# Attention and gated FFN on one core: the pass for the score maxima by single PSUM banks, the end with turned sums, and the orders of a period refitted

## The reference

```
q = rotary(xn @ wq + bq), k = rotary(xn @ wk + bk), v = xn @ wv + bv     16 query heads, 2 groups of k and v, 16 wide
attention = softmax(q k^T / 16) v @ wo + bo                              over 1024 keys
ffn = fwht(silu(xn @ W1^T) * (xn @ W3^T)) @ W2^T                         1024 hidden units, fwht = normalised Walsh-Hadamard
```

## Time and profile before

| | us |
|---|---|
| median of 3 runs | 1078.76 |
| lowest, highest | 1078.07, 1084.82 |
| profiled execution, its own time | 1075.6 |
| its span | 1073.8 |
| PE, VectorE, ScalarE, GpSimd busy | 1014.3, 771.2, 707.5, 347.2 |
| granted share of the TensorE clock, mean | 0.99 |

### The profile page before, as it was taken

One profiled execution on the slowest core, in us unless ns is written; L12 is line 12 of the kernel. 1 busy time (PEld: TensorE's weight loads), 2 busy tenths in 40 slices (PEclk: granted clock), 3 DMA queues, 4 the chain that ended last, 5 costly groups with the idle time before them and its releaser, 6 DMA issues.

```text
span 1073.8 us, 19578 instructions
## 1 busy us (share of the span) xinstructions
PE 1014.3 (94%) x7604; PEld 549.6 (51%) x7604; DVE 771.2 (72%) x934; ACT 707.5 (66%) x1336; POOL 347.2 (32%) x300
## 2 busy tenths in 40 slices
PE   4889999999999999999999999999999999999997
PEld 3554445545554555545554455545555454644454
DVE  5996688677776778767786777767776778776723
ACT  4256677657765777657776577667775678566873
POOL 5262722073312634054310735126320224012300
PEclk9998999999999999999999999999999999999999
DMA  8762155212052253402242250521123131510001
GB/s 234 177 172 75 53 137 104 74 57 86 17 117 78 76 136 66 100 21 84 64 103 74 97 126 18 117 64 51 51 62 71 33 83 33 111 32 6 12 8 50
DMA packets 64941, 84.03 MB, mean 78 GB/s; under 512 B 19960, under 2 KB 34168, under 8 KB 64848
## 3 DMA queue, kind: packets, MB, share of 16 engines
q1 hardware_dynamic: 63296, 80.74, 29.1%
q10 hardware_dynamic: 1552, 2.03, 0.7%
HBM read 54.97 MB, written 22.51 MB: 72 GB/s over the span
## 4 chain that ended last, share of the span: by engine, by line
PE 66%; DVE 17%; ACT 5%; issue 4%; DMA 4%; SPq 3%; POOL 2%; DVEq 0%; ACTq 0%; POOLq 0%
PE ps L1501 16%; PE ps L1558 14%; PE ps L1545 13%; DVE negpart L1295 11%; PE ps L1456 9%; PE ps L1513 8%; PE ps L1467 3%; DVE hid L1267 3%; PE ps L1434 3%; ACT work L1079 2%; DMA qk_parts<-hid 1%; DMA xn<-in_x 1%; SPq L776 1%; SPq L784 1%; DMA recip_rows<-dens 1%
## 5 line engine op out<-in xcount | busy, mean ns | idle before, releaser
L1295 DVE TENSOR_REDUCE negpart<-ps 128x2 f32<-128x1024 f32 x512 | 619.0, 1224 | 235.7 <-PE ps L1456 234.8
L1079 ACT ACTIVATE work<-ps 128x512 f32<-128x512 f32 x1024 | 560.0, 603 | 262.3 <-PE ps L1545 256.9
L1558 PE MATMUL ps<-work,vb 128*32 128x512 f32 x2048 | 274.6, 609 | 5.8 <-ACT osum L1090 5.0
L1545 PE MATMUL ps<-qh,kb 50*128 50x512 f32 x1024 | 265.1, 450 | 10.3 <-ACT work L1079 7.4
L1456 PE MATMUL ps<-kb,qh 48*128 48x512 f32 x1024 | 226.8, 433 | 9.6 <-DVE negpart L1295 5.3
L1545 PEld LDWEIGHTS ps<-qh,kb 50*128 50x128 f32 x1024 | 123.4, 185 | 212.3 <-ACT work L1079 159.0
L1501 PE MATMUL ps<-xf,w_p 64*128 64x512 f32 x1536 | 218.3, 400 | 7.4 <-DVE negpart L1295 1.4
L1501 PEld LDWEIGHTS ps<-xf,w_p 64*128 64x128 f32 x1536 | 143.6, 185 | 49.7 <-DVE hid L1267 16.3
L933 POOL TENSOR_TENSOR hid_p<-hid,hid_p 128x512 fp32r<-128x512 f32 x64 | 82.2, 1286 | 203.1 <-ACT hid_p L1068 203.1
L1456 PEld LDWEIGHTS ps<-kb,qh 48*128 48x128 f32 x1024 | 98.1, 185 | 82.7 <-DVE negpart L1295 48.4
L1513 PEld LDWEIGHTS ps<-w2t_p,hid_p 64*128 64x128 f32 x1536 | 107.7, 185 | 34.2 <-DVE negpart L1295 27.1
(11 more groups left out here) (125 smaller groups left out, 484.6 us busy)
## 6 DMA issues: line engine op xcount, KB each, us to landing
xf<-xn_parts SPq DMA_DIRECT2D x32, 512.0 KB, 8.5
qh<-qk_parts SPq DMA_DIRECT2D x192, 64.0 KB, 2.3
xn_parts<-xt SPq DMA_DIRECT2D x14, 512.0 KB, 3.5
qh<-mturned SPq DMA_DIRECT2D x256, 2.0 KB
y<-in_x SPq DMA_DIRECT2D x8, 512.0 KB, 4.8
attnt<-osum SPq DMA_DIRECT2D x124, 32.0 KB, 2.0
recips<-recip_rows SPq DMA_DIRECT2D x120, 32.0 KB, 1.8
xn<-in_x SPq DMA_DIRECT2D x7, 512.0 KB, 5.0
```

The costliest lines, as they stand in the source:

```text
L1079: nc.scalar.activation(prob[(ITSTEPS * i + j) % NPROB][:, h, :], ps[:, 4 + u % 3, :], ACT.Exp, scale=SCALE).then_inc(exp_done, 1)
L1295: nc.vector.tensor_reduce(negpart[a][:, f, :, h, t, e], two(slot), AX.X, ALU.max, negate=True).then_inc(ring_free[slot], 1)
L1545: pe.matmul(ps[:, 4 + u % 3, :], kb[i % 2][rows, kt * P:(kt + 1) * P], qh[2 * a + f][rows, h, :], start=True, stop=True).then_inc(s2_done, 1)
L1558: m = pe.matmul(ps[VW * h:VW * (h + 1), 7, :], vb[b % 2][g][:, kt, :], prob[(ITSTEPS * i + j) % NPROB][:, h, :], start=(kt == 0), stop=(kt ...
```

## The change

1. **Maxima by single banks.** An S1 entry has two pieces, two fills and two frees. Piece 0 is the product for r = 1, piece 1 that for r = 0. Each fills one bank; VectorE takes one maximum of 128x512 for each, in the same order. Piece 0 waits only for the first free of an S1 unit before it in the slot, piece 1 for the second.
2. **Other products between them.** `first(slot, *halves)` issues the named pieces, so that `first(1, 0)`, something else, `first(1, 1)` puts scores or own pieces between the two products of a unit.
3. **Orders refitted.** PE's order of each kind of period is written anew, and where exponentials, tanh, copies and saves lie on ScalarE. VectorE's order in a period is the same, with two maxima for each unit.
4. **Last iteration.** UP ends at period 9, DN runs in periods 11 to 14, and period 15 (WOz) projects the first half of iteration 7's own sums. Reciprocals of half 0 are taken at period 12 there.
5. **The end.** The last copy of the sums, `select` and `chosen` go. VectorE turns the sums out of PSUM in blocks of 32x32 (queries onto partitions), takes reciprocals of 128x8, multiplies, turns back; both in halves of 256. PE gathers the four head blocks' output in banks 2 to 5: first the part of the normalised half from `attnt`, then the part of the turned one, against rows of `wo` (`wo_last`, zero in the denominators' rows; a memset on GpSimd and four DMAs in iteration 6). Two additions of 128x512 follow.

The diff, cut to its core (kinds WO, XT, None, WOx, QKx, UPxo and the first two periods of the kernel are rewritten in the same manner):

```diff
 def up_at(i):
-    return range(4, 12) if i + 2 < NBLK else (1, 2, 3, 5, 6, 7, 8, 10)
+    return range(4, 12) if i + 2 < NBLK else (1, 2, 3, 5, 6, 7, 8, 10 if i + 1 < NIT else 9)
+def down_at(i):
+    return range(12, 16) if i + 1 < NIT else range(11, 15)
...
-PIECES = {"XT": 2, "QK": 4, "Q2": 2, "WO": 4, "UP": 4, "DN": 4, "VT": 1, "S1": 1}
-FULLS = {"XT": 2, "QK": 2}
-FREES = {"XT": 2, "UP": 2, "VT": 2}
+PIECES = {"XT": 2, "QK": 4, "Q2": 2, "WO": 4, "UP": 4, "DN": 4, "VT": 1, "S1": 2}
+FULLS = {"XT": 2, "QK": 2, "S1": 2}
+FREES = {"XT": 2, "UP": 2, "VT": 2, "S1": 2}
...
         if kind in ("UP", "UPo"):
-            own(0, 1)
-            first(1)
+            own(0)
+            first(1, 0)
+            own(1)
+            first(1, 1)
             scores(0)
             sums_before()
+            first(1, 0)
             scores(1)
-            first(1)
-            own(2)
+            first(1, 1)
+            own(2, 3)
+            first(1, 0)
             scores(2)
-            own(3)
-            first(1)
+            first(1, 1)
             sums(i, 2 * p)
+            first(1, 0)
             scores(3)
-            first(1)
+            first(1, 1)
         elif kind in ("DN", "DNo"):
             scores(0)
-            first(0)
-            first(1)
+            first(0, 0, 1)
+            first(1, 0, 1)
             sums_before()
-            own(0)
             scores(1)
-            first(1)
+            own(0)
+            first(1, 0)
             own(1)
+            first(1, 1)
             scores(2)
+            first(1, 0)
             own(2)
-            first(1)
-            scores(3)
+            first(1, 1)
             own(3)
+            scores(3)
             sums(i, 2 * p)
...
         elif kind == "QK":
+            first(1, 0)
             scores(0)
-            first(1)
-            first(0)
+            first(1, 1)
             scores(1)
+            first(0, 0, 1)
+            sums_before()
+            sums(i, 2 * p)
             scores(2)
-            sums_before()
-            own(0)
-            first(1)
-            own(1, 2, 3)
-            first(1)
-            sums(i, 2 * p)
+            first(1, 0, 1)
+            own(0, 1, 2)
+            first(1, 0)
             scores(3)
+            first(1, 1)
+            own(3)
             extra()
...
+        elif kind in ("WO", "WOo"):
+            first(1, 0), scores(0), first(1, 1), scores(1), first(1, 0), scores(2), first(1, 1)
+            own(0, 1, 2, 3), scores(3), first(1, 0, 1), sums_before(), first(0, 0, 1), sums(i, 2 * p)
+        elif kind == "XT":
+            first(1, 0), scores(0), first(1, 1), own(0, 1), scores(1), first(1, 0, 1), sums_before()
+            scores(2), first(1, 0), scores(3), first(1, 1), first(0, 0, 1), sums(i, 2 * p)
...
-                dve.wait_ge(*filled(("S1", i, a, u)))
...
-                nc.vector.tensor_reduce(negpart[a][:, f, :, h, t, e], two(slot), AX.X, ALU.max,
-                                        negate=True).then_inc(ring_free[slot], 1)
+                for n, r in enumerate((1, 0)):
+                    dve.wait_ge(*filled(("S1", i, a, u), n + 1))
+                    nc.vector.tensor_reduce(negpart[a][:, f, r, h, t, e:e + 1], two(slot)[:, r, :], AX.X, ALU.max,
+                                            negate=True).then_inc(ring_free[slot], 1)
...
-                if k == 0 and RING[entry][2] > 0:
+                if k == 0 and RING[entry][3] > 0:
+                    pe.wait_ge(ring_free[slot], RING[entry][3])
+                if k == 1 and RING[entry][2] > RING[entry][3]:
                     pe.wait_ge(ring_free[slot], RING[entry][2])
...
-                    for r in range(ROWT):
-                        rows = slice(GRP * r, GRP * r + SROWS)
-                        m = pe.matmul(bank[:, r, :], ...)
+                    r = ROWT - 1 - k
+                    rows = slice(GRP * r, GRP * r + SROWS)
+                    m = pe.matmul(bank[:, r, :], ...)
+                    done = True
...
                     if kind == "UP":
                         exponentials(i, j, 0, 4)
                         hidden_before(i, p)
+                        gate(i, up_at(i).index(p))
                         exponentials(i, j, 4, 5)
-                        gate(i, up_at(i).index(p))
-                        exponentials(i, j, 5, 6)
                         linear(i, up_at(i).index(p))
-                        exponentials(i, j, 6, 8)
+                        exponentials(i, j, 5, 8)
...
+            for n, cols in enumerate(halves):
+                nc.vector.transpose(last_sums[:, cols], ps[:, 7, cols]).then_inc(last_turned, 1)
+            for n in range(2):
+                nc.vector.reciprocal(shares[n], blocks[n][:, :, HD]).then_inc(last_step, 1)
+            for n in range(2):
+                nc.vector.tensor_tensor(blocks[n][:, :, 0:HD], blocks[n][:, :, 0:HD],
+                                        shares[n].unsqueeze(2).broadcast_to([P, 2 * P // VW, HD]), ALU.mult).then_inc(last_step, 1)
+            for n, cols in enumerate(halves):
+                nc.vector.transpose(last_attn[:, cols], last_sums[:, cols]).then_inc(last_norm, 1)
```

More of the change, by code:

```diff
@@ L135, in sums_before, with first @@
             sums(i - 1, ITSTEPS - 1)
-    def first(slot):
+    def first(slot, *halves):
         nonlocal unit
[L139 to L142, removed]
+        for n in halves:
+            at = i + unit // (2 * UNITS)
+            if at < NIT:
+                piece(("S1", at, unit // UNITS % 2, unit % UNITS), n, slot)
+            unit += n
     def own(*numbers):
@@ new lines, in walk_iteration @@
+            own(3)
+            scores(3)
+            extra()
+            first(1, 0, 1)
+        elif kind == "UPxo":
+            first(0, 0, 1)
+            first(1, 0)
+            scores(0)
+            first(1, 1)
+            scores(1)
+            own(0)
+            first(1, 0)
+            scores(2)
+            first(1, 1)
+            own(1, 2)
+            scores(3)
+            own(3)
+            first(1, 0, 1)
+            sums_before()
+            extra()
+            sums(i, 2 * p)
+        elif kind == "Nos":
+            first(0, 0)
+            scores(0)
+            first(0, 1)
+            sums_before()
+            scores(1)
+            scores(2)
+            first(0, 0)
+            scores(3)
+            first(0, 1)
+            first(1, 0, 1)
+            sums(i, 2 * p)
+            first(0, 0, 1)
+        elif kind == "Not":
+            first(1, 0)
+            scores(0)
+            first(1, 1)
+            scores(1)
+            first(0, 0)
+            scores(2)
+            first(0, 1)
+            scores(3)
+            first(1, 0, 1)
@@ L265, in walk_iteration @@
             sums_before()
-            first(0)
-            first(1)
+            first(1, 0, 1)
+            sums(i, 2 * p)
+        elif kind == "WOz":
             scores(0)
             scores(1)
-            own(0, 1, 2, 3)
+            own(0, 1)
             scores(2)
-            sums(i, 2 * p)
-            first(1)
+            own(2, 3)
             scores(3)
[L275 to L297, removed]
@@ L342, in walk_opening, with walk_closing @@
         piece(("UP", 0, c), k, 2 + c % 2)
-def walk_closing(sums, piece, select):
+def walk_closing(sums, piece, last_values):
     sums(NIT - 1, ITSTEPS - 1)
-    select()
-    for half in range(QB):
-        for k in range(4):
-            piece(("WO", NIT - 1, half), k, 1 - half)
+    last_values()
 def ring_table():
-    full, free, at = [0] * 4, [0] * 4, {}
+    full, free, at, before = [0] * 4, [0] * 4, {}, [None] * 4
     def count(entry, k, slot):
         if k == 0:
-            at[entry] = (slot, full[slot], free[slot])
+            at[entry] = (slot, full[slot], free[slot], free[slot] - (entry[0] == before[slot] == "S1"))
+            before[slot] = entry[0]
             full[slot] += FULLS.get(entry[0], 1)
@@ L1197, in _ @@
+                        exponentials(i, j, 4, 5)
+                        linear(i, up_at(i).index(p))
+                        exponentials(i, j, 5, 8)
+                    elif kind == "DNo":
+                        exponentials(i, j, 0, 1)
+                        hidden_before(i, p)
+                        exponentials(i, j, 1, 3)
+                        save_finished(i, p)
+                        exponentials(i, j, 3, 8)
+                    elif kind == "WOo":
                         exponentials(i, j, 0, 4)
@@ L1424, in _ @@
-            projected_sums(NIT - 1, 0)
-            for n in range(2):
-                at = y[:, (NBLK - 1) % 2, 2 * n:2 * n + 2, :].rearrange("p t d -> p (t d)")
-                dve.wait_ge(*filled(("WO", NIT - 1, 1), n + 1))
-                nc.vector.tensor_tensor(at, at, two(0)[:, n, :], ALU.add).then_inc(ring_free[0], 1)
+            halves = [slice(n * 2 * P, (n + 1) * 2 * P) for n in range(2)]
+            blocks = [last_sums[:, cols].rearrange("p (j c) -> p j c", c=VW) for cols in halves]
```

243 lines of the change are left out of this document (118 added, 125 removed).

## The result

| | before | changed |
|---|---|---|
| median of the runs | 1079.63 | 1095.25 |
| lowest, highest | 1078.07, 1084.82 | 1087.58, 1098.10 |
| profiled execution, span | 1075.6, 1073.8 | 1092.8, 1091.0 |
| mean granted clock, profiled execution | 0.990 | 0.955 |

In 37 other executions of the kernel before (1075.8 to 1088.9 us) the mean clock was 0.976 to 0.989, in 32 of them 0.984 or less, so the profiled one, at 0.990, is among its fastest. The ratio is 1.012 (95% interval 1.008 to 1.016): slower by about 1%, where 1041 us and faster were forecast, and outside the range of 1020 to 1072.

What follows compares the result with a forecast made beforehand. PE and VectorE were taken to wait for each other in a loop through one buffer. Terms of -22.5 - 3.8 - 10.7 - 2.5 - 4.5 + 1.7 = -42.3, plus 5 for what was missed, gave -37: 1041 us, range 1020 to 1072.

Steps and rivals of the forecast that it cites:

- XT + QK: XT and QK periods of a steady iteration: about 6.3 and 10.9 us, together 17.2, for 15.94 and 1.4 moved in.
- WO + WOx: WO and WOx periods of a steady iteration: 7.8 and 9.3 us, together 17.1, for 17.98.
- UP: UP periods of a steady iteration: 7.35 us each for 7.58, counted as 7 x 7.35 + 5.5.
- DN: DN periods of a steady iteration: 7.45 us each, four taking 29.8 for 32.93, of which 1.4 moves into the next period.
- Q2's stall: QK period: Q2 writes the slot the second projection must read first, a stall of 1.05 us.
- the gated product's: UP periods: VectorE's late gated product leaves PE a stall of 0.27 us, plus 0.10.
- (d): Rival: each split product shows a weight load, 390 x 0.10 = +39, no change, 1080 us; chance 0.05.
- The opening: 24 units back to back, where the split maxima are not hidden: 24 x 0.07 = +1.7 us.
- The end: From the last sums to the end of the last addition: 5.3 us for 9.83, so -4.5.
- (b): Rival: the new orders eat the gain through waits in Q2, scores and periods, 30 us back, 1070 us; chance 0.20.
- (c): Rival: a single product leaves the other row half idle, 390 x 0.23 = +90 for -37, 1130 us; chance 0.05.
- (a): Rival: the refit clears the gated wait too, UP periods come to 6.98 us, -20, 1020 us; chance 0.18.

Runs made afterwards that it cites:

- e1: Changed kernel with SyncE's eight loads of the next iteration's first maxima put ahead of spreading the reciprocals: 1044.7 us, 0.968 of the kernel before.
- e3: Kernel before with split products and split maxima alone, both products together where the pair was, old orders and old end: 1087.49 us, 1.007.
- e6: Changed kernel with the 2 MB load of the turned x moved from ahead of the reciprocals to behind the maxima's loads: 1050.01 us, 0.969.
- e8: Changed kernel, maxima's loads between the reciprocals' write and the wait for it, both products of a unit together at the second's place: 1082.96 us, 1.000.
- e9: Changed kernel, maxima's loads between the reciprocals' write and the wait for it, one QK sums moved between own(3) and extra(): 1041.74 us, 0.962.
- e10: e9 with the gated product between the third unit's maxima and, between UP periods, the fourth unit's second product behind the next own(0): 1039.29 us, 0.959.
- e5: Kernel before with the six loads of queries put ahead of the eight loads of the first maxima on SyncE: 1147.53 us, 1.062.
- e2: Kernel before with the same swap as e1, the first maxima's loads ahead of spreading the reciprocals: 1079.25 us, 0.998.

## Why the prediction was wrong, point by point

**Steps that held.** For a steady iteration, forecast against e1, where the border is cured: XT + QK 17.2 and 16.95; WO + WOx 17.1 and 17.08; UP 57.0 and 57.41; DN 29.8 and 29.60 (there by an offset: 7.9 for the first and 7.2 for the others, where each was put at 7.45); sum 121.1 and 121.0. The maxima are 0.685 us long and two take 1.29, so 0.60 apart. Q2's stall and the gated product's are where they were put. The mechanism of the split was read rightly. e1's 1044.7 lies 4 us from the forecast, with some luck: from the last DN period of iteration 5 to the end e1 gains 14.0 us on the profiled kernel before, where the sum has 19.2 (10.7, the 1.5 counted elsewhere, 2.5 and 4.5), and the 5 us added for what was missed cover just that.

Two arguments of the prediction have to be put right. The Trainium skill (VectorE: DVE Perf Modes, "The DRAIN you can't avoid") goes on, behind the sentence that the prediction cites, with an exception: "A next op that is not held starts earlier", held being its word for one that starts only when all earlier ones have finished. Starts 1.131 us apart at a length of 1.23, and 0.60 apart at 0.685, agree with that exception, so the trace does not disagree with the section as a whole.

The other is that on weight loads in the same rows, against rival (d). The six full-height products 0.22 apart in the earlier trace rows have 256 columns, and pairs of DN products of as many columns stand 0.12 apart there, so that row by itself leaves time for a load in the open. What bears the argument out are the products of the projection in QK of the kernel before, also full-height, each with its own load, and of 512 columns:

```profile
460.09 1.22 PEld L1434 LDWEIGHTS ps<-xt,wqkv_p 128*128 128x128 f32 x6 [0.25 <-issue]
460.09 1.67 PE L1434 MATMUL ps<-xt,wqkv_p 128*128 128x512 f32 x6
```

Six take 1.67 us, just what six pairs of half-height UP products take behind a stall, 0.23 apart, and their first and last load lie within 1.22 us: no load between them shows. What holds the products of 256 columns at 0.22 is open.

**The step that failed** is DN: "Four take 29.8". They would have, but the end of an iteration is not PE's alone. I followed what PE, VectorE and ScalarE hand each other, and costed SyncE by what the edit adds to it ("on a queue with gaps"). I never asked what that queue delivers at the border and by when. Counted from the write of the reciprocals, the border came 1.3 us sooner (2.5 at the last two), and the chain that the maxima's loads stand behind (write, landing, eight spreading DMAs) did not get shorter with PE's periods but 2.2 us longer, for the most part because the write moved closer behind the turned x. The kernel before met this date within 0.4 us at five borders of seven. Here PE stood still for 2.4 to 4.7 us at each border, 23.8 in all, and the last DN period came to 10.1 to 12.4 us instead of 7.2.

**The clock, not in the sum at all.** The mean granted clock of 0.955 means some 98 us at 1.2 GHz of 1091 (2 x 0.045 x 1091), against 21 in the profiled execution before and 46 in e1. With a stall of 2.4 to 4.7 us at a border it fell for 3 to 14 us, at three of them once more within the iteration, and XT, QK and WO then ran at half speed. A stall on PE thus cost about twice its length: 1091.0 minus 1043.9 is 47 us over seven borders, 6.7 each, 3.4 of them stall. The other 23 us would be, by this working, the price of the 52 us more at half the clock (98 less 46). Part of the clock's falls is not of this kind. The changed kernel has one of 17 us in the opening, near 45 us, about 1 us behind a gap of 2.05 us without products, and e1, e3, e6, e8, e9 and e10 have it too. So does e5, with the old units. The profiled execution of the kernel before has a gap of 1.87 us there and no such fall. So it isn't a matter of single banks. Nor does the kernel seem to settle it: ten executions of e2, old units too, have a clock of 0.991 to 0.992 (two of them, at 1074.4 and 1074.8 us) or 0.980 to 0.986 (eight, at 1078.1 to 1083.3); what falls in those eight no trace shows. What decides it was not tried.

**The opening** cost 5.3 us (first score at 78.4 for 73.1), where +1.7 was forecast. This fall of the clock is enough for all of it: e5, with the old maxima and the same fall, has its first score at 78.6, and the runs with single maxima and this fall have it at 77.2 to 78.9. So the +1.7 for the split maxima does not show in any run.

**The end** held within a little. In the changed kernel:

```profile
1082.61 0.13 PEld L1596 LDWEIGHTS ps<-work,vb 128*32 128x32 f32 x4 [0.30 <-issue]
...
1083.72 0.78 DVE L1452 STREAM_TRANSPOSE work<-ps 128x256 f32<-128x256 f32 x2 [1.94 <-PE ps L1596]
1084.42 0.31 DVE L1455 RECIPROCAL work<-work 128x8 f32<-128x8 f32 x2
1084.66 0.46 DVE L1458 TENSOR_TENSOR work<-work 128x128 f32<-128x128 f32 x2
...
1087.62 0.69 DVE L1466 TENSOR_TENSOR y<-y,ps 128x512 f32<-128x512 f32 x1 [0.18 <-PE ps L1611]
```

The last `sums` begins with the load at 1082.61 and the last addition ends at 1088.31: 5.7 us, forecast 5.3, before 9.83. The turns take 0.78 a pair, where 0.75 was put; the reciprocals and products 0.31 and 0.46, where 0.4 and 0.5 were put.

**The rivals.** None was the one that came, and none had the time: the nearest, (d), was put at 1080. The sign named for (b), iterations of 124 us and more, did appear (127.9 from 586.08 on), and yet not for its reason: it put the loss into PE's orders. (c) and (d) are out: e1's UP periods of 7.38 leave no room for 0.11 a split. (a) did not come true either; e10 shows that the gated wait is not the only one between 7.38 and 6.98. The iterations with WOo (6 and 7) were off as well: WOo takes 10.0 in e1 at its shortest, and I had 8.2.

## What to carry to other kernels

Before a stretch is made shorter, list all that is due at its end, DMAs that another queue issues above all, and take from the trace how long before its use each arrives; a row with a wait of 0.3 us for a DMA, or a last issue that is always just one landing ahead, is a date that is met by chance. A small load that something waits for goes ahead of the large one that is needed later, and the write whose landing the queue itself waits for goes there too, as long as the large one still comes in time (e6). When a gain doesn't show, compare the same stretches by period kind before doubting the edit: here the eight UP periods had their gain all along (57.41 us for 58.75), and two swapped calls brought the rest.

## What the runs showed that was not expected

Stalls of PE for 2.4 to 4.7 us came with half the granted clock for 3 to 14 us at a time; in e5, with stalls of 5.1 us at six borders and 3.9 at the last, it was 7 to 21 us, and 17 or more at four of the seven. A write of 16 KB took 6.3 to 9.3 us to land behind 2 MB that were still under way (kernels before and after), 1.4 to 3.1 with the 2 MB behind it (e6), and 1.4 to 2.4 where they had landed by then (e1). Splitting a reduction of 128x1024 in two cost 0.07 us on VectorE (0.60 + 0.60 against 1.13 apart), and a lone half-height product between pairs cost PE nothing that the periods show.
